# A four-network graph kernel on one Trainium2 core: products of the last network moved to GpSimd

## The reference

```python
x1 = x_nodes[src].reshape(-1, N_SEG, EXTENT)
x2 = x_edges.reshape(-1, N_SEG, EXTENT)
i1, i2, i3 = (path_indices[:, 0], path_indices[:, 1], path_indices[:, 2])
contrib = path_coeffs[None, :, None] * x1[:, i1, :] * x2[:, i2, :]
edge_out = jnp.zeros((x2.shape[0], N_SEG, EXTENT), x_nodes.dtype).at[:, i3, :].add(contrib)
out = jnp.zeros((n_nodes, OP_SIZE), x_nodes.dtype).at[dst].add(edge_out.reshape(-1, OP_SIZE))
```

## Time and profile before

| | |
|---|---|
| median of 3 runs | 840.88 us (839.43 to 841.88) |
| the profiled execution | 840.28 us |
| its span, first to last instruction | 838.5 us |
| TensorE busy in matmuls | 784.4 us, 94% |
| VectorE busy | 601.4 us, 72% |
| ScalarE busy | 220.0 us, 26% |
| GpSimd busy | 126.9 us, 15% |
| mean granted TensorE clock | 0.989 |

### The profile page before, as it was taken

The page is one execution under the profiler, slowest core; times in us unless marked ns, Lnnn a source line. Parts: engine busy times, 40 slices in busy tenths (PEclk is TensorE's granted clock), DMA queues, the critical chain, the costliest instruction groups (busy, mean ns, idle before and its releaser), DMA issues.

```text
span 838.5 us, 11005 instructions
## 1 busy us (share of the span) xinstructions
PE 784.4 (94%) x3172; PEld 530.8 (63%) x3172; DVE 601.4 (72%) x1575; ACT 220.0 (26%) x458; POOL 126.9 (15%) x150
## 2 busy tenths in 40 slices
PE   6889999999898999999999999889999999999978
PEld 3557667667566666667567564566686685685753
DVE  8776676675686544453553563789999999999995
ACT  7623123123121311311311312403404304305200
POOL 5000000000101000000000001611441361441000
PEclk9999999999999999999999999899999999999989
DMA  4912333323131433333342100751632443330000
GB/s 167 347 63 102 113 103 110 113 82 131 63 134 64 162 113 126 119 113 121 118 146 80 63 1 25 228 173 51 200 102 80 138 134 104 111 88 0 1 0 25
DMA packets 39335, 88.39 MB, mean 105 GB/s; under 512 B 3986, under 2 KB 4319, under 8 KB 39295
## 3 DMA queue, kind: packets, MB, share of 16 engines
q1 hardware_dynamic: 34656, 72.72, 25.4%
q0 software_dynamic: 4640, 15.21, 6.1%
HBM read 86.86 MB, written 1.05 MB: 105 GB/s over the span
## 4 chain that ended last, share of the span: by engine, by line
PE 74%; DVE 14%; issue 5%; DVEq 3%; ACT 2%; POOL 1%; ACTq 0%; another core or an unknown queue 0%; POOLq 0%
PE PS L764 44%; PE PS L1085 15%; PE PS L1071 11%; DVE big L1539 2%; PE PS L773 2%; DVE tail L1530 1%; PE PS L936 1%; DVE x L1602 1%; PE PS L885 1%; DVEq L1502 1%; PE PS L799 1%; DVEq L1506 1%; DVE big L1226 1%; PE PS L981 1%; DVE big L1276 1%
## 5 line engine op out<-in xcount | busy, mean ns | idle before, releaser
L764 PE MATMUL PS<-big 128*128 128x512 f32 (+1 forms) x368 | 137.1, 524 | 1.7 <-DVE big L1430 1.7
L1530 DVE SCALAR_TENSOR_TENSOR tail<-big,coef 128x448 f32 (+3 forms) x208 | 125.2, 614 | 5.0 <-issue 4.7
L1539 DVE TENSOR_TENSOR big<-big,tail 128x448 f32 (+3 forms) x208 | 115.3, 554 | 3.6 <-DVE tail L1530 2.4
L764 PEld LDWEIGHTS PS<-big 128*128 128x128 f32 x368 | 67.4, 190 | 63.4 <-issue 54.8
L764 PE MATMUL PS<-hT,big 128*128 128x256 f32 (+1 forms) x512 | 87.0, 329 | 4.4 <-ACT hT L687 4.4
L585 POOL DMA_INDIRECT big<-h_rows,src_i x58 | 75.1, 1295 | 83.4 <-PE PS L1071 60.8
L764 PEld LDWEIGHTS PS<-hT,big 128*128 128x128 f32 x512 | 77.5, 191 | 15.2 <-ACT hT L687 7.3
L555 POOL TENSOR_TENSOR rstd<-var,minus_half 128x1 f32<-128x1 f32 x34 | 20.5, 605 | 409.9 <-DVE var L1136 409.8
L1071 PE MATMUL PS<-big,hotd_more 128*128 128x512 f32 x152 | 66.0, 592 | 0.0
L1085 PE MATMUL PS<-hotd_more,tail 128*128 128x256 f32 x280 | 64.6, 386 | 0.0
L1085 PEld LDWEIGHTS PS<-hotd_more,tail 128*128 128x128 f32 x280 | 54.6, 195 | 7.9
(11 more groups left out here) (210 smaller groups left out, 1110.1 us busy)
## 6 DMA issues: line engine op xcount, KB each, us to landing
big<-in_edge_attr_dram SPq DMA_DIRECT2D x32, 512.0 KB, 3.5
big<-in_L_gnn_vn_W_dram SPq DMA_DIRECT2D x12, 1024.0 KB, 5.4
big<-in_L_gnn_m_w_dram SPq DMA_DIRECT2D x8, 1024.0 KB, 5.3
big<-in_L_gnn_gcn_W_dram SPq DMA_DIRECT2D x7, 1024.0 KB, 5.2
big<-in_L_gnn_wv_dram SPq DMA_DIRECT2D x4, 1024.0 KB, 5.3
big<-in_L_gnn_wq_dram SPq DMA_DIRECT2D x4, 1024.0 KB, 5.0
big<-in_L_gnn_wk_dram SPq DMA_DIRECT2D x4, 1024.0 KB, 5.1
big<-in_L_gnn_wo_dram SPq DMA_DIRECT2D x4, 1024.0 KB, 5.3
```

The costliest lines, as they stand in the source:

```text
L764: return pe.matmul(o, lhsT, rhs, start=start, stop=stop)
L1530: dve.scalar_tensor_tensor(out=prod[:, slot, tiles, :], in0=xs[:, tiles, bass.ds(i1, EXT)], scalar=coef[:, row:row + 1], in1=xe[:, tiles, ...
L1539: dve.tensor_tensor(o, o, prod[:, slot, tiles, :], ALU.add)._wait_ge(path_step, max(product_at[slot], added_at[0])).then_inc(path_step, 1)
```

## The change

In groups 1 to 4 GpSimd makes the products of all sets but the first (`POOL_SETS`), with the same four multiplications a set as VectorE's; VectorE makes the first set of each group and all eight of group 0. The sets are 8, 6, 5, 5, 4 instead of 8, 7, 6, 6, 4, and the rows that no longer are in a set are summed rows: 32, 40, 44, 44, 48. TensorE waits for GpSimd's sets by a new semaphore, `pool_ready`, and so do the zeroing of a group's sums and the load of its edges. GpSimd makes the first of its sets of a group ahead of the next group's gathers, the others behind them. The gathers start tile by tile as TensorE frees their tiles, where they waited for all. At the end the placement of the turned sets alternates between two targets, x and h (which ScalarE zeroes in group 2), and VectorE adds h to x afterwards. A zeroing of one PSUM bank by VectorE is replaced by the start flag of the first matmul.

```diff
-ORDER = [[0, 1, 2, 3, 4, 5, 6, 7], [1, 2, 0, 3, 4, 5, 6, 7], [2, 0, 3, 1, 4, 5, 6, 7], [2, 0, 3, 1, 4, 5, 6, 7],
+ORDER = [[0, 1, 2, 3, 4, 5, 6, 7], [2, 0, 3, 1, 4, 5, 6, 7], [3, 0, 4, 1, 5, 6, 7, 2], [3, 0, 4, 1, 5, 6, 7, 2],
-SETS_OF = [8, 7, 6, 6, 4]
+SETS_OF = [8, 6, 5, 5, 4]
+POOL_SETS = [(), (1, 2, 3, 4, 5), (1, 2, 3, 4), (1, 2, 3, 4), (1, 2, 3)]
...
+                sp.wait_ge(pool_ready, POOL_AT[g - 1])
                 edge_group(g)
...
+            def make_set(g, i):
+
+                k, at, n = SETS - SETS_OF[g] + i, SET_AT[g] + i, SIZES[g]
+                pool.load(places, path[0:1, 3 * BLOCK_ROWS * k:3 * BLOCK_ROWS * k + 3 * 4])
+                if at >= 2:
+                    pool.wait_ge(set_used, at - 1)
+                for q in range(4):
+                    i1, i2 = (pool.snap(r, min_val=0, max_val=(SEGS - 1) * EXT) for r in places[3 * q:3 * q + 2])
+                    ins = pool.tensor_tensor(prods[at % 2][:, 0:n, q * EXT:(q + 1) * EXT],
+                                             part[SOURCE_AT[g]][:, 0:n, bass.ds(i1, EXT)],
+                                             part[EDGE_AT[g]][:, 0:n, bass.ds(i2, EXT)], ALU.mult)
+                ins.then_inc(pool_ready, 1)
...
-            fetch_sources(0)
+            for j in range(BY_PE, SIZES[0]):
+                fetch_source(0, j)
             pool.wait_ge(picked, BY_PE)
-            fetch_sources(1)
+            for j in range(3):
+                fetch_source(1, j)
+            pool.wait_ge(setcoef_set, 1)
+            for j in range(3, SIZES[1]):
+                fetch_source(1, j)
             for g in range(1, GROUPS):
                 pool.wait_ge(path_step, STEP_AT[g])
+                pool.wait_ge(pool_ready, POOL_AT[g])
                 zero_sums(g)
+                group_in(g)
+                make_set(g, POOL_SETS[g][0])
                 if g + 1 < GROUPS:
-
-                    pool.wait_ge(tile_summed, START[g])
-                    fetch_sources(g + 1)
+                    for j in range(SIZES[g + 1]):
+                        pool.wait_ge(tile_summed, min(START[g - 1] + j + 1, START[g]))
+                        fetch_source(g + 1, j)
+                for i in POOL_SETS[g][1:]:
+                    make_set(g, i)
...
                 act.wait_ge(path_step, STEP_AT[g])
+                act.wait_ge(pool_ready, POOL_AT[g])
                 zero_sums(g)
+                if g == 2:
+                    act.wait_ge(h_kept, 16 * NT)
+                    act.wait_ge(picked, BY_PE)
+                    act.activation(h[:].rearrange("p t d -> p (t d)"), zero.to_broadcast([P, NT * D]),
+                                   ACT.Copy).then_inc(spare_zero, 1)
...
-                pe.wait_ge(set_ready, n + 1)
+                if i in POOL_SETS[g]:
+                    pe.wait_ge(pool_ready, POOL_AT[g] + POOL_SETS[g].index(i) + 1)
+                else:
+                    pe.wait_ge(set_ready, OWN_AT[g] + sum(o not in POOL_SETS[g] for o in range(i)) + 1)
...
-                if j == 2:
-                    dve.wait_ge(picked_kept, 2)
-                    dve.memset(set_bank(3), 0.0).then_inc(picked_kept, 1)
...
-                    if has_set:
+                    makes = has_set and k - (SETS - SETS_OF[g]) not in POOL_SETS[g]
+                    if makes:
                         while waiting:
                             add_product(*waiting.pop(0))
                         set_rows(k, rows)
...
                 for q in range(4):
-                    o = x[:, :, bass.ds(bounded(set_regs[4 * k + q]), EXT)]
-                    link(dve.tensor_tensor(o, o, turned[:, :, q * EXT:(q + 1) * EXT], ALU.add))
+                    n = 4 * at + q
+                    if n >= 2:
+                        dve.wait_ge(placed, n - 1)
+                    o = (h if q % 2 else x)[:, :, bass.ds(bounded(set_regs[4 * k + q]), EXT)]
+                    dve.tensor_tensor(o, o, turned[:, :, q * EXT:(q + 1) * EXT], ALU.add).then_inc(placed, 1)
+            dve.wait_ge(placed, 4 * SETS)
+            for t in range(NT):
+                ins = dve.tensor_tensor(x[:, t, :], x[:, t, :], h[:, t, :], ALU.add)
+            link(ins)
```

More of the change, by code:

```diff
@@ L37 @@
 SETS = PATHS // BLOCK_ROWS
-ORDER = [[0, 1, 2, 3, 4, 5, 6, 7], [1, 2, 0, 3, 4, 5, 6, 7], [2, 0, 3, 1, 4, 5, 6, 7], [2, 0, 3, 1, 4, 5, 6, 7],
+ORDER = [[0, 1, 2, 3, 4, 5, 6, 7], [2, 0, 3, 1, 4, 5, 6, 7], [3, 0, 4, 1, 5, 6, 7, 2], [3, 0, 4, 1, 5, 6, 7, 2],
          [4, 0, 5, 1, 6, 2, 7, 3]]
-SETS_OF = [8, 7, 6, 6, 4]
+SETS_OF = [8, 6, 5, 5, 4]
+POOL_SETS = [(), (1, 2, 3, 4, 5), (1, 2, 3, 4), (1, 2, 3, 4), (1, 2, 3)]
+POOL_AT = [sum(map(len, POOL_SETS[:g])) for g in range(len(POOL_SETS) + 1)]
 SUMMED_OF = [PATHS - 4 * n for n in SETS_OF]
@@ L44 @@
 SET_AT = [sum(SETS_OF[:g]) for g in range(GROUPS + 1)]
+OWN_AT = [SET_AT[g] - POOL_AT[g] for g in range(GROUPS + 1)]
 STEP_AT = [2 * sum(SUMMED_OF[:g]) for g in range(GROUPS)] + [2 * sum(SUMMED_OF) + 2 * SPLIT_ROWS]
@@ L329, in gnn_stack_kernel @@
             sem, ["h_ready", "hot_squared", "hotd_ready", "acc_zero", "path_step", "tile_summed", "final"])
+        spare_zero, placed = sem("spare_zero"), sem("placed")
+        pool_ready = sem("pool_ready")
         node_summed = sem("node_summed")
@@ L579, in zero_sums, with fetch_source, group_in @@
                 pool.memset(part[SUM_AT[g]][:, ZERO_CUT:SIZES[g], :], 0.0).then_inc(acc_zero, 1)
[L581 to L587, removed]
+            def fetch_source(g, j):
+                tile = START[g] + j
+                pool.indirect_dma_start(out=part[SOURCE_AT[g]][:, j, :], out_offset=None, in_=h_rows,
+                                        in_offset=bass.IndirectOffsetOnAxis(ap=src_i[:, tile:tile + 1], axis=0)
+                                        ).then_inc(x1_in[g], 16)
+            places = [pool.alloc_register(f"place{i}") for i in range(3 * 4)]
+            def make_set(g, i):
[9 more added lines that the diff above has]
+                ins.then_inc(pool_ready, 1)
+            def group_in(g):
+                pool.wait_ge(x2_in[g], 16 * (SIZES[g] // PIECE))
+                pool.wait_ge(x1_in[g], 16 * (SIZES[g] - (0 if g else BY_PE)))
             pool.wait_ge(alpha_done, 2)
@@ L1085, in sum_set @@
                     ins = pe.matmul(set_bank(SETS - SETS_OF[g] + i), prods[n % 2][:, j, :], hotd(j),
-                                    start=g == 0 and j == 0 and SETS - SETS_OF[g] + i != 3, stop=True,
-                                    skip_group_check=True)
+                                    start=g == 0 and j == 0, stop=True, skip_group_check=True)
                 ins.then_inc(set_used, 1)
@@ L1497, in _, with load_block @@
             loads = []
-            def load_block(k):
+            def load_block(g, k):
                 into = regs[len(loads) % 2]
                 loads.append(k)
-                dve.load(into, path[0:1, 3 * BLOCK_ROWS * k:3 * BLOCK_ROWS * (k + 1)])
+                lo = 3 * 4 if k - (SETS - SETS_OF[g]) in POOL_SETS[g] else 0
+                dve.load(into[lo:], path[0:1, 3 * BLOCK_ROWS * k + lo:3 * BLOCK_ROWS * (k + 1)])
                 return into
@@ L1508, in block_behind @@
             def block_behind(g, at):
-                return ORDER[g][at + 1] if at + 1 < len(ORDER[g]) else (ORDER[g + 1][0] if g + 1 < GROUPS else None)
-            loaded = load_block(ORDER[0][0])
+                return (g, ORDER[g][at + 1]) if at + 1 < len(ORDER[g]) else ((g + 1, ORDER[g + 1][0]) if g + 1 < GROUPS else None)
+            loaded = load_block(0, ORDER[0][0])
             for j in range(BY_PE):
@@ L1514, in _ @@
                 dve.tensor_copy(part[SOURCE_AT[0]][:, j, :], PS[:, 2 + j, :]).then_inc(picked_kept, 1)
-                if j == 2:
-                    dve.wait_ge(picked_kept, 2)
-                    dve.memset(set_bank(3), 0.0).then_inc(picked_kept, 1)
-            dve.wait_ge(picked_kept, BY_PE + 1)
+            dve.wait_ge(picked_kept, BY_PE)
             for g in range(GROUPS):
@@ L1573, in _ @@
                         if behind is not None:
-                            loaded = load_block(behind)
+                            loaded = load_block(*behind)
                     if g == GROUPS - 1 and at >= len(ORDER[g]) - 2:
-                        if behind is not None and not has_set:
-                            loaded = load_block(behind)
+                        if behind is not None and not makes:
+                            loaded = load_block(*behind)
                         split += [(BLOCK_ROWS * k + i, rows[i]) for i in range(4 if has_set else 0, BLOCK_ROWS)]
@@ L1583, in _ @@
                         summed_row(BLOCK_ROWS * k + i, every, *rows[i])
-                        if i == 5 and behind is not None and not has_set:
-                            loaded = load_block(behind)
+                        if i == 5 and behind is not None and not makes:
+                            loaded = load_block(*behind)
```

(1 more changed line is left out.)

## The result

The changed kernel takes 868.3 us (median of 4 runs, 867.21 to 869.0) against 841.38 us before (839.43 to 842.4, 4 runs): a ratio of 1.0322, 95% interval 1.0299 to 1.0344. It is slower by 27 us, where 870 was forecast. The profiled execution took 868.09 us, its span 866.3.

What follows compares the result with a forecast made beforehand. TensorE and VectorE, level in the last network, were taken as the bound. Profiled 840.28 us + 28 (VectorE's loss to GpSimd beyond its saving) + 2.2 (TensorE's slow clock) - 0.2 (placement) = 870.3, stated as 870; range 819 to 876.

Steps and rivals of the forecast that it cites:

- The bound: Last network, groups 1 to 3: TensorE bounds, VectorE just as full, so both must shrink and GpSimd must disturb neither.
- The slip: VectorE's delay per GpSimd product beside it: 0.81 to 0.98 us for 448 elements, 0.71 to 0.84 for 384.
- rows 7: First-stage profile rows: a 128-element GpSimd product delays VectorE's comparisons 0.27 to 0.28 us; scaled by elements, 0.98 at 448.
- The groups: Last network, groups 1 to 4: VectorE needs 49.6, 54.3, 54.3 and 49.1 us before GpSimd's disturbance is added.
- part 2: Sets moved to GpSimd in groups 1 to 4: with the added summed rows, VectorE saves 28.1 us, at 2.14 us a set.
- TensorE's clock at the end: Last part of the last network: after idling, TensorE's first matmuls run at 1.2 instead of 2.4 GHz, costing 2.2 us.
- Part 5: Final placement with two targets: perhaps 5 us less, but covered by TensorE's last 10.4 + 10.5 us; at most 0.2 us gained.
- The gathers: Next group's gathers on GpSimd: 1.295 + 0.30 us each, hidden; TensorE waits about 5 us in group 1, covered by VectorE.
- The hidden parts: Two placement targets and gathers by tile: both covered by other work, at most about 0.2 us from the targets.
- Side by side: Rival: GpSimd and VectorE run without holding each other up, TensorE bounds, 818 to 829 us; chance 0.27.
- sharing in part: Rival: GpSimd and VectorE partly share, delay 0.3 to 0.6 us a product, 831 to 849 us; chance 0.11.
- The third: Rival: GpSimd gets in too rarely, 8.6 us a set, TensorE waits, 876 us; chance counted within the lock forecast's 0.62.

## Why the prediction was right, point by point

**The bound.** That VectorE and TensorE were level, and that what is taken off VectorE must not come back as a disturbance, held. The write-only run shows the gain there was to have at most: 821 us.

**The slip.** Forecast 0.81 to 0.98 us for 448 elements and 0.71 to 0.84 for 384, from a slip of 0.28 us at 128 elements. Measured 0.90 at 448. At 384, with VectorE's usual 0.50 us between starts, the timeline of group 4 has 1.27:

```profile
816.85 1.35 DVE L1569 SCALAR_TENSOR_TENSOR tail<-big,coef 128x384 f32 x1
818.12 1.35 DVE L1578 TENSOR_TENSOR big<-big,tail 128x384 f32 x1
819.39 1.35 DVE L1569 SCALAR_TENSOR_TENSOR tail<-big,coef 128x384 f32 x1
```

0.77 us. With 0.43 at 224 the slip grows by about 2.1 ns an element with no fixed part; the proportional reading of rows 7 was the right form, and a little high. That a slip of one-input bf16 comparisons would carry over to two-input f32 instructions was an assumption; it held. 52 x 0.90 + 12 x 0.77 = 56.0 us, against the forecast's 50.6 to 61.0, whose middle is 55.8. The lines view confirms it: 128 products and 128 additions of 14 tiles at 0.854 and 0.804 us in the mean, where before's 116 of each had 0.676 and 0.617, are 128 x 0.178 + 128 x 0.187 = 46.7 us for 52 GpSimd products, 0.90 each.

**The groups.** The prediction's terms give 65.8 to 69.2 for group 1 (49.6 and 20 slips), 67.3 to 70.0 for groups 2 and 3, 57.6 to 59.2 for group 4. Measured 66.7, 67.8, 68.1 and 57.4. Together 24.6 us more, where the middle said 28. With slips of 56.0 us, VectorE was relieved of 31.4 us and not of 28.1: the term that was 3 us off is the saving of part 2. Against the run in which VectorE makes all sets, groups 1 to 3 show it: 185.9 + 46.8 - 202.6 = 30.1 us for 13 sets, 2.3 us each instead of 2.14.

**TensorE's clock at the end.** Forecast 2.2 us; the last part took 1.8 us more in all, with the 0.3 us that VectorE's earlier end gives back in it:

```profile
839.89 9.26 PE L1109 MATMUL PS<-big,xn 128*128 128x512 f32 x16 [9.02 <-DVE big L1578]
848.99 3.60 PE L1109 MATMUL PS<-big,hotd_more 128*128 128x512 f32 x8
```

After 9.02 us without work the first 16 matmuls took 9.26 us instead of 7.13: the granted clock was 0.53 from 839.89 to 844.50, near the 1.2 GHz level, and 1.00 after it. Part 5 of the prediction has the last stretch of the kernel before as 10.4 + 10.5 us; its rows give 10.6 + 10.5, which changes nothing in the sum.

**The gathers.** Here a size was off. They were taken at 1.295 us, and TensorE to wait about 5 us for the second GpSimd set in group 1. It waited 12.27:

```profile
622.12 3.77 PE L1126 MATMUL PS<-xn,tail 128*128 128x256 f32 x8 [12.27 <-POOL tail L603]
```

The gathers for groups 2 to 4 took 1.668 us in the mean, eight of the 14 in group 1 about 1.96, the upper end of the earlier trace rows. The same 40 gathers had 1.409 us in the kernel before; the 1.295 is a mean that takes in the 18 of the first two groups. They had 1.516 us with the gathers by tile alone, and 1.620 where VectorE makes the changed kernel's sets. What changed is what lies beside them. In the kernel before, the eight gathers that run wholly beside a set of VectorE took 0.99 us in the mean, the 18 beside summed rows alone 1.49. One gather beside rows, up to the set at 683.61, and one within that set:

```profile
681.90 1.96 POOL L585 DMA_INDIRECT big<-h_rows,src_i  x1 [0.30 <-issue]
683.61 2.27 DVE L1549 TENSOR_TENSOR prods<-big 128x448 f32 x4
684.16 0.95 POOL L585 DMA_INDIRECT big<-h_rows,src_i  x1 [0.30 <-issue]
```

Now they all lie beside summed rows. Both kinds of VectorE work have two operands in SBUF, so the count of operands does not tell why the rows hold up a gather and the sets do not; that stays open. It cost nothing, because VectorE ended the group later still, as the prediction said it would; in the write-only run, where TensorE bounds, it did cost 5.8 us.

**Not foreseen: 1.4 us in group 0.** VectorE started its fourth set at 551.32 instead of 549.92, after a pause of 1.99 us instead of 0.48, with nothing in the records that it could have waited for. The end of group 0 goes with the chip and not with the kernel: it lies between 577.0 and 578.2 us in the six profiles of experiments from two of the chips, and between 579.4 and 580.3 in the four from the third, where the kernel before with one hidden part alone has it too. So the 1.4 of the 27.8 us of the two spans need not be the change's; what causes the pause stays open.

**What was luck.** The terms that the prediction names came to 24.6 + 1.8 = 26.4 us, where it had 30.0. The 1.4 us that it did not foresee bring the total closer to the forecast than its terms are.

**The hidden parts.** The two targets and the gathers by tile were forecast at nothing, and are nothing, each measured alone.

**The rivals.** Side by side (818 to 829 us) falls with the stretched rows; sharing in part, a slip of 0.3 to 0.6 us, falls with the measured 0.90. Whether 0.90 us is the whole of GpSimd's reading time no run shows directly; that it grows with the elements and vanishes without reads speaks for it. The third, GpSimd starved, falls as well: a set of 14 tiles took 5.5 to 6.3 us and not 8.6, and one VectorE instruction goes by for each GpSimd one. That it can't be worth it follows from the numbers: a GpSimd set costs VectorE 4 x 0.90 = 3.6 us and saves it 2.14 to 2.3.

## What to carry to other kernels

Before work is moved from VectorE to an idle GpSimd, count the operands in SBUF on both sides: if VectorE's instructions have two and GpSimd's read, expect the moved work to hold VectorE up, here by 3.6 us for 2.14 to 2.3 us saved. A stage in which two engines are level gains only as much as the less relieved of them, and a run in which the moved work only writes tells what it would be worth at most without the disturbance. A wait of the level partner, such as the 5.8 us of TensorE here, is a better place to move work to than an engine that looks idle.

## What the runs showed of the hardware

A GpSimd product of two f32 operands holds up VectorE's two-operand instructions by 0.43, 0.77 and 0.90 us at 224, 384 and 448 elements, a copy of 448 by 0.33, and a write by 0.01 to 0.02 at most. With two-operand instructions on both sides the two engines take turns, instruction by instruction (four in 5.66 and four in 5.84 us). What I had not expected is how much it gives back when every second VectorE instruction has one operand: with the statistics in place of the additions a GpSimd product cost 0.35 us instead of 0.90, and a gather's issue 1.014 us in the mean instead of 1.668, near the 0.95 it takes undisturbed. Whether an addition with one operand in PSUM would do the same in a complete kernel was not tried.
